# One GNN layer on one core: edge sums spilled to DRAM and scattered during the node stage

## What is computed

```
deg         = max(number of edges that end in the node, 1)
edge_weight = 1 / sqrt(deg[src] * deg[dst])
edge_msg    = relu(edge_attr @ W1e + b1e) @ W2e + b2e
messages    = (x[src] + edge_msg) * edge_weight
agg         = segment_sum(messages, dst)
h           = relu(((1 + gin_eps) * x + agg) @ W1n + b1n) @ W2n + b2n
o           = h + x
o           = o / sqrt(mean(o^2) + eps) * rms_w
out         = layernorm(x + o)
```

## Time and profile before

| | us |
|---|---|
| median of 3 runs | 1851.71 |
| lowest and highest run | 1847.68, 1855.45 |
| span of the profiled execution, first to last instruction | 1621.4 |
| between the span and the median | 230.3 |

### The profile page before, as it was taken

The page is one execution under the profiler, slowest core; times in us unless marked ns, Lnnn a source line. Parts: engine busy times, 40 slices in busy tenths (PEclk is TensorE's granted clock), DMA queues, the critical chain, the costliest instruction groups (busy, mean ns, idle before and its releaser), DMA issues. The chain is left out here.

```text
span 1621.4 us, 33827 instructions
## 1 busy us (share of the span) xinstructions
PE 1376.2 (85%) x7563; PEld 865.4 (53%) x7563; DVE 1294.2 (80%) x4160; ACT 1050.1 (65%) x3889; POOL 1309.6 (81%) x2146
## 2 busy tenths in 40 slices
PE   7995899888878888887878781499999999999993
PEld 4553455444434344443434340377777777777772
DVE  8999798767766766676666672099999999999998
ACT  7995254444444344344344342299999999999997
POOL 7777777777777777777777777369999999999997
PEclk9998899988999898899988895699999999999997
DMA  9999332222222222222222411436777777677763
GB/s 345 378 376 387 117 97 68 68 79 80 67 67 67 69 88 70 67 67 67 80 80 68 157 42 40 145 131 245 291 264 289 264 279 277 267 291 267 290 254 152
DMA packets 63860, 275.61 MB, mean 170 GB/s; under 512 B 17737, under 2 KB 20211, under 8 KB 39344
## 3 DMA queue, kind: packets, MB, share of 16 engines
q1 hardware_dynamic: 38066, 230.80, 38.1%
q0 software_dynamic: 25136, 43.60, 9.2%
q10 hardware_dynamic: 590, 0.53, 0.1%
HBM read 154.37 MB, written 128.19 MB: 174 GB/s over the span
## 5 line engine op out<-in xcount | busy, mean ns | idle before, releaser
L600 POOL DMA_INDIRECT xs<-in_x,src_x x391 | 393.5, 1006 | 119.3 <-issue 104.8
L607 POOL DMA_INDIRECT agg_scratch<-scaled,sca_i x390 | 392.8, 1007 | 118.8 <-issue 106.3
L1157 PE MATMUL bank<-digits,picks 128*128 128x512 f16 x1568 | 414.4, 412 | 0.0
L731 ACT ACTIVATE scaled<-sums,dd 128x128 f32<-128x128 f32 x390 | 124.5, 390 | 442.8 <-DMA agg_scratch<-scaled,sca_i 442.8
L641 POOL TENSOR_SCALAR xsc<-xn,rms 128x128 f32<-128x128 f32 x784 | 277.5, 371 | 61.9 <-issue 18.1
L963 DVE SCALAR_TENSOR_TENSOR sums<-sums,cont,weights 128x128 f32<-128x128 f32 x391 | 135.1, 345 | 235.8 <-issue 218.2
L943 DVE SCALAR_TENSOR_TENSOR picked<-iota_h,src_lo,bank 128x512 f16<-128x512 f16 x392 | 288.6, 737 | 9.1 <-PE bank L1157 8.2
L779 ACT ACTIVATE squares<-res 128x128 f32<-128x128 f32 x784 | 257.6, 437 | 0.0
L1157 PEld LDWEIGHTS bank<-digits,picks 128*128 128x128 f16 x1568 | 165.0, 105 | 172.5 <-issue 49.9
L655 POOL TENSOR_SCALAR on<-z,neg_mean,rstd 128x128 f32<-128x128 f32 x564 | 244.3, 443 | 0.0
L1214 PEld LDWEIGHTS bank<-w2n,hn 128*128 128x128 f32 x1568 | 205.8, 191 | 70.5 <-issue 64.6
(11 more groups left out here) (153 smaller groups left out, 2336.1 us busy)
## 6 DMA issues: line engine op xcount, KB each, us to landing
agg_scratch<-zeros SPq DMA_DIRECT2D x48, 1024.0 KB
xn<-in_x SPq DMA_DIRECT2D x48, 1024.0 KB, 8.8
out<-on SPq DMA_DIRECT2D x48, 1024.0 KB, 4.9
ag<-agg_scratch SPq DMA_DIRECT2D x47, 1024.0 KB, 6.8
highq<-src_high_scratch SPq DMA_DIRECT2D x24, 512.0 KB, 3.9
ea<-in_edge_attr SPq DMA_DIRECT2D x21, 512.0 KB, 3.7
xs<-in_x,src_x POOLq DMA_INDIRECT x391, 2.7
agg_scratch<-scaled,sca_i POOLq DMA_INDIRECT x390, 2.2
```

The lines of the kernel that those rows point to most:

```text
L600: pool.indirect_dma_start(out=xs[:, b % XS, j, :], out_offset=None, in_=x, in_offset=bass.IndirectOffsetOnAxis(ap=src_x[:, t:t + 1], axis= ...
L607: pool.indirect_dma_start(out=agg_rows, out_offset=bass.IndirectOffsetOnAxis(ap=sca_i[:, t:t + 1], axis=0), in_=scaled[:, b % SR, j, :], i ...
L1157: last = pe.matmul(ps[COUNTS[tile]][:, :], picks[:, s, c, tile * P:(tile + 1) * P], digits[:, c, :, :].rearrange("p d l -> p (d l)"), star ...
```

## The change

The edges are cut into seven groups of 56 tiles (`G`, `GT`), the group with the highest nodes first; the edge list is padded to 392 tiles. ACT no longer hands `scaled` to POOL: it stores each batch (256 KB) to a DRAM tensor `sums_scratch` with a DMA of its own queue. POOL issues all gathers in the edge stage and, beside the last 48 batches of them, 135 scatters; the others come after. A scatter reads from `reload`, two buffers of 16 tiles, which POOL fills with a plain DMA (`refill`). Behind each group comes its own join, an adding scatter of one row a partition; their sums are made on PE and scaled by ACT at the end of the edge stage.

Node blocks run from the highest nodes down. SP loads the sums of a block once as many joins have landed as the table `waits_i` says for it, which DVE computes from `dst`. For the first 98 of 196 steps (`BOTH`) POOL takes no part: DVE makes `z` straight from `xn` and `rms` in four tile operations, and `on` tiles 0 and 1; ACT makes tiles 2 and 3. From step 98 on POOL makes `xsc` and `on` as before.

The degree look-up is turned round: nodes' low parts select (two comparisons in place of four), and the sixteen matmuls of a batch have 391 columns; `picked` has 391 too. DVE's edge batches run in a loop of eight (`Fori`), PE's and ACT's too; SP's node blocks are unrolled. The run lists are made before the counting, and for all seven groups, with one round trip through DRAM (`ends_scratch`). The cut diff:

```diff
+    G, GB = 7, 14
+    GT = GB * TB
+    BATCHES = G * GB
+    T = BATCHES * TB
...
+    RB = 4 * TB
+    RELOADS = -(-T // RB)
+    EARLY = 4
...
+    LONE, ROUND = 34, SPB * XR
+    BOTH = LONE + 4 * ROUND
+    SA, SF = BOTH - 7, BOTH - 18
...
+    sums_d = nc.dram_tensor("sums_scratch", (BATCHES * P, TB * D), f32)
...
+        def act_tiles(m, w):
+            B = m // SPB
+            return (2, 3) if w < SF or isinstance(B, int) and (SPLIT <= B < BLOCKS - 2 or B == BLOCKS - 1) else (3,)
+
+        def main_tiles(m, w):
+            B = m // SPB
+            return (0, 1) if w < SF or isinstance(B, int) and B >= SPLIT else (0, 1, 2)
+
+        def late_tiles(B):
+            return (2,) if B == BLOCKS - 2 else (0, 1)
...
+            for s in range(SR):
+                sp.wait_ge(stored[s], stores(s, (G - 1) * GB))
+            sp.dma_start(tails[:, :, :], bass.AP(sums_d, ((GB - 1) * P * TB + TB - 1) * D,
+                                                 [[TB * D, P], [GB * P * TB * D, G - 1], [1, D]])).then_inc(tails_in, 16)
...
+            def load_x(i):
+                need(sp, z_ready, (i - XR + 1) * SPB)
+                sp.dma_start(xn[:, i % XR, :, :], in_group_order(x, i)).then_inc(xn_in[i % XR], 16)
+
+            def load_sums(i):
+
+                joins = sp.value_load(waits_i[0:1, i:i + 1], min_val=16, max_val=16 * G)
+                need(sp, cT_done, (i - AR + 1) * SPB)
+                sp.wait_ge(fin_added, joins)
+                sp.dma_start(ag[:, (i + 1) % AR, :, :], in_group_order(agg_d, i)).then_inc(ag_in[(i + 1) % AR], 16)
+
...
+            for i in range(XR):
+                load_x(i)
+            load_sums(0)
+            load_sums(1)
+            sp.wait_ge(msg_ready, BATCHES)
...
+            def gather(b):
+                if b == XS - TEMPS:
+                    pool.wait_ge(lists_ready, 1)
+                if b < XS - TEMPS:
+                    need(pool, counted, min(BATCHES, b * TB - COUNT_LEAD))
+                elif b < XS:
+                    need(pool, m_done, b - (XS - TEMPS) - MIX_LEAD)
+                else:
+                    pool.wait_ge(msg_ready, b - XS + 1)
...
+                for j in range(TB):
+                    t = b * TB + j
+                    pool.indirect_dma_start(out=xs[:, b % XS, j, :], out_offset=None, in_=x,
+                                            in_offset=bass.IndirectOffsetOnAxis(ap=src_x[:, t:t + 1], axis=0)
+                                            ).then_inc(xs_in[b % XF], 16)
+
+            def refill(q):
+                batches = min((q + 1) * RB, T) // TB
+                for s in range(SR):
+                    pool.wait_ge(stored[s], stores(s, batches))
+                need(pool, scattered[q % 2], 16 * scatters(q))
+                n = batches - q * RB // TB
+                pool.dma_start(reload[:, q % 2, 0:n * TB, :].rearrange("p (b j) d -> p b (j d)", j=TB),
+                               bass.AP(sums_d, q * P * RB * D, [[TB * D, P], [P * TB * D, n], [1, TB * D]])
+                               ).then_inc(reloaded[q % 2], 16)
+
+            def scatter(t):
+                q, c = t // RB, t % RB
+                if c == 0:
+                    pool.wait_ge(reloaded[q % 2], 16 * (q // 2 + 1))
+                if t % GT < GT - 1:
+                    pool.indirect_dma_start(out=agg_rows,
+                                            out_offset=bass.IndirectOffsetOnAxis(ap=sca_i[:, t:t + 1], axis=0),
+                                            in_=reload[:, q % 2, c, :], in_offset=None,
+                                            bounds_check=N - 1, oob_is_err=False).then_inc(scattered[q % 2], 16)
+                if c == RB // 2 and q + 1 < RELOADS:
+                    refill(q + 1)
+
+            def last_block(r):
+                return ((r + 1) * GT - 1) // RB
+
+            def join(r):
+
+                for k in (last_block(r), last_block(r) - 1):
+                    pool.wait_ge(scattered[k % 2], 16 * scatters(k + 2))
+                pool.wait_ge(fin_scaled, r + 1)
+                need(pool, fin_added, 16 * r)
+                pool.indirect_dma_start(out=agg_rows, out_offset=bass.IndirectOffsetOnAxis(ap=fin_i[:, r:r + 1], axis=0),
+                                        in_=joined[:, r, :], in_offset=None, bounds_check=N + P - 1,
+                                        oob_is_err=True, compute_op=ALU.add).then_inc(fin_added, 16)
...
+            BEFORE, BESIDE = 10, 135
+            for b in range(XS, BATCHES):
+                gather(b)
+                if b == XS:
+                    for k in range(ZERO_AHEAD):
+                        pool.wait_ge(agg_zeroed[k], 16 * len(range(k, ZERO_DMAS, ZERO_AHEAD)))
+                done, parts = max(b - XS - BEFORE, 0), BATCHES - XS - BEFORE
+                if b == XS + BEFORE:
+                    refill(0)
+                for t in range(done * BESIDE // parts, (done + 1) * BESIDE // parts if b >= XS + BEFORE else 0):
+                    scatter(t)
+            for t in range(BESIDE, T):
                 scatter(t)
...
+                for r in range(G - 1):
+                    if t == max(BESIDE + 12 + r, (last_block(r) + 1) * RB + 3):
+                        join(r)
+            join(G - 1)
...
+            node_step(BOTH - 1, BOTH - 1)
+            pool.wait_ge(mean_ready, SF // SPB + 1)
+            pool.wait_ge(rstd_ready, SF // SPB + 1)
+            pool.wait_ge(on_main, SF)
+            for n in range(run(pool, BOTH, 6, ROUND, node_step), STEPS + 15):
+                node_step(n, n)
...
+                m, s = b - 6, (u - 6) % SR
+                if live(m, BATCHES):
+                    act.wait_ge(scaled_ready, at(m + 1))
+                    act.dma_start(sums_d[:, :].rearrange("(b p) c -> b p c", p=P)[bass.ds(at(m), 1), :, :].rearrange(
+                        "b p c -> p (b c)"), scaled[:, s, :, :].rearrange("p j d -> p (j d)")).then_inc(stored[s], 16)
...
+                if b == BATCHES:
+                    act.wait_ge(fin_summed, EARLY)
+                    for r in range(EARLY):
+                        join_scale(r, ps[2], r)
+                if b == BATCHES + 2:
+                    act.wait_ge(fin_summed, G - 1)
+                    for r in range(EARLY, G - 1):
+                        join_scale(r, ps[3], r - EARLY)
+            act.wait_ge(fin_summed, G)
+            join_scale(G - 1, ps[7], 0)
...
+            def degree(b, u, j):
                 if j == 0:
-                    dve.wait_ge(first_counted, b + 1)
+                    dve.wait_ge(first_counted, at(b + 1))
                     need(dve, ds_ready, b - DR + 1)
                 if j == TB // 2:
-                    dve.wait_ge(second_counted, b + 1)
...
+                return dve.scalar_tensor_tensor(picked[:, j, :], iota_h[:, 0:PICK], column(src_hi, b * TB + j),
+                                                ps[COUNTS[j]][:, 0:PICK], ALU.is_equal, ALU.mult,
+                                                accum_out=deg[:, u % DR, j:j + 1])
...
+            with dve.Fori(0, 11) as i:
+
+                slot = nc.s_assert_within((i + 1) * XF - ((i + 1) * 13 >> 6) * XS, 0, XS - XF,
+                                          skip_runtime_bounds_check_because="13 * k >> 6 is k // 5 for k up to 11")
+                for u in range(10, 10 + XF):
+                    edge_step(Count(i, XF, u), u, slot + (u - 10))
+            for b in range(10 + 11 * XF, BATCHES + 4):
+                edge_step(b, b, (b - 2) % XS)
...
+            def finish(m, w, tiles, finished):
+                v, B, o, h = w % ZR, m // SPB, w // SPB % OR, w % SPB * TB
+                if h == 0:
+                    dve.wait_ge(rstd_ready, at(B + 1))
+                    dve.wait_ge(mean_ready, at(B + 1))
+                    need(dve, out_sent[o], B // OR * 16)
+                for j in tiles:
+                    last = dve.tensor_scalar(on[:, o, h + j, :], z[:, v, j, :], neg_mean[:, v // SPB, h + j:h + j + 1],
+                                             rstd[:, v // SPB, h + j:h + j + 1], ALU.add, ALU.mult)
+                last.then_inc(finished, 1)
...
                     dve.wait_ge(res_ready, at(m + 1))
-                    need(dve, z_ready, m)
-                    dve.tensor_tensor(ps[7][:, :], res[:, s, :, :].rearrange("p j d -> p (j d)"), ps[6][:, :],
+                    if both:
+                        dve.wait_ge(z_ready, at(m))
+                    q = ps[7][:, :] if both else xsc[:, s % 2, :, :].rearrange("p j d -> p (j d)")
+                    dve.tensor_tensor(q, res[:, s, :, :].rearrange("p j d -> p (j d)"), ps[6][:, :],
                                       ALU.mult).then_inc(q_ready, 1)
...
+                    need(dve, on_act, m - ZR + 1)
+                    if both:
+                        need(dve, on_main, m - ZR + 1)
+                        dve.wait_ge(xsc_ready, at(m - SA + 1))
+                        dve.tensor_tensor(z[:, v, :, :].rearrange("p j d -> p (j d)"), ps[7][:, :],
```

(58 more changed lines are left out.)

975 lines of the change are left out of this document (479 added, 496 removed).

## The result

The changed kernel takes 2060.5 us in the median of three runs (2054.6 to 2062.8), where the kernel before takes 1851.7: a ratio of 1.111, with a 95% interval of 1.106 to 1.115. It is slower by 209 us; 1648 was predicted. Its profiled execution took 2060.48 us and spans 2058.7: only 1.8 us lie around the span.

A forecast was written before the change was run, and what follows sets the result against it. POOL's gather and scatter count was taken to bound the edge stage. First `res` at 755, plus 577.7 of node stage and 85 of added DVE work, gave 1418 us of span; with 230.3 around it, 1648 (range 1600 to 1725).

The forecast's parts named there:

- The surroundings of the span: Whole run: 230.3 us between profiled span (1621.4) and median (1851.71), unexplained by any view, were carried over unchanged.
- POOL's instruction count, not its busy share, is the edge bound: Edge stage before: POOL issues without a break, 1.305 us per gather or scatter, holding messages 8.29 us apart.
- Edge pace 5.36: Edge stage after: PE sets the pace, 6.16 less 0.8 us for narrower pick matmuls, 5.36 us a batch.
- the new prelude: Before the first batch: more input DMAs and group work start batches 10 us later, bounds 3 and 20.
- Refills and POOL's count: Edge stage: 367 issues at 1.305 us and 9 refills at 2 us put POOL's last gather at about 721.
- First `res`: Turn to the node stage: join 0 at about 739, first result at 755 instead of 1044, 289 us gained.
- 98 node steps without POOL: First half of node stage: DVE takes over `z` and two `on` tiles, adding 85 us, bounds 45 and 135.
- The scatters are hidden with 20 us to spare: Beside node steps: POOL finishes 240 scatters, 15 refills, 6 joins at 1097; DVE wants `xsc` at 1117.
- (a): Rival: POOL is late at the switch to `xsc`, ending near 1190; about 1720 us, chance 0.14.
- (b): Rival: edge stage keeps 6.16 us a batch as DVE or ACT takes PE's place; 1726 us, chance 0.12.
- (c): Rival: new tiles cost 0.195 us, giving 1608; time around the span may shrink, another 29 off; chance 0.09.
- (d): Rival: slower than before, scatters beside node steps bind at 2.3 us spacing, or start waits for all joins (2006); chance 0.05.

The follow-up runs named there:

- b_same: The kernel before, unchanged, run and profiled again: 1854.7 us.
- a_480: Kernel after, 480-wide POOL write behind every scatter and gathers from batch 32, waiting for the previous write; POOL in node steps from 114: 1645.4 us, ratio 0.888 to before.
- a_every4: Kernel after, with a small POOL write and a wait for it behind each fourth gather or scatter only: 1876.0 us.
- a_drain: Kernel after, with a four-element POOL write and a wait for it behind every gather and scatter: 1749.2 us.
- a_no_late_scatters: Kernel after without its 250 scatters from tile 135 on; sums incomplete: 1751.8 us.
- a_plain_late: Kernel after, its 250 scatters from tile 135 on sent as plain POOL DMAs of the same rows to a spare tensor: 1764.7 us.
- a_long_lag1: Kernel after, with a 480-wide POOL write behind every gather and scatter, POOL waiting for the write before it: 1720.4 us, ratio 0.922 to before.
- a_240: As a_480, but writes of 240 elements and POOL taken into the node steps from step 98: 1762.8 us, ratio 0.950 to before.

## Why the prediction was wrong, point by point

**The surroundings of the span (first step): wrong.** "230.3 us lie around the span ... I carry them over unchanged." They were no overhead but stalls inside timed executions which the profiled one didn't have; b_same has 1.7 us around its span. This was the warning that I read over. Carrying them over took them as fixed; they grew with what POOL issued beside the others.

**"POOL's instruction count, not its busy share, is the edge bound": right for the profiled execution only.** In b_same POOL gets out 374 instructions in the 600 us, 1.60 us apart, and what ACT waits for is "remote". With that, relieving POOL of 255 scatters there could not give 2.93 us a batch: from b_same to the kernel after the pace didn't change at all (10.5 to 10.7 over messages 17 to 65).

**Edge pace 5.36: mechanism right, where it can be seen.** 5.40 with POOL silent, 5.39 in a_480, with PE full. That agrees with what was said of the 391 columns, though no run has 512 beside them. But the term was applied to all 98 batches. The last message came at 1084.4, not 720, of which 49 us are the late start (249.0, not 200). Against b_same's 250.0 the new prelude costs nothing, where 10 us were allowed.

**Refills and POOL's count: the issues near, the end not.** A refill's issue is 0.83 us, not 2. POOL's last gather came at 852, not 721: it waited for messages (99.9 us from 300 to 800), that is, for stalled engines. Then it stood idle for 208.8 us until join 0's row was scaled: the late scatters waited for the join though nothing in them needs it. The forecast had the two ends coincide.

**First `res`: 1100.0, not 755;** from join 0, at 1083.7, it took 16.3 us, in line with the 13.5 and the 3 for the larger load. The edge part gained 1270.2 - 1100.0 = 170 us on b_same, against 289 forecast.

**98 node steps without POOL: right in kind, and to the us by luck.** Without late scatters the stage lasts 664.1 us (1748.7 - 1084.6), 86 more than b_same's 578.1; 85 was the sum. But the first 98 steps give 76 of it: the 80 steps with two `on` tiles take 3.72 us, not 3.79. Another 11 come from the second half, 286.3 us from its first `res` to the last against 275.5 in b_same, which the forecast left as it was.

**"The scatters are hidden with 20 us to spare": this failed step decides the sign.** POOL did its 239 scatters behind join 0 in 344 us (1083.7 to 1427.9), faster than the 358 forecast and as undisturbed as its row promised. The prediction took the overlap as free: it asked only when POOL would be done, and put what the scatters cost PE, DVE and ACT at nothing. They cost 958.6 - 664.1 = 295 us, in about 14 steps. The balance against b_same closes: -170.2 + 380.5 = 210.3 us, the difference of the spans; 380.5 is 86 of work moved to DVE and 295 of stall.

Why is it so much worse than in the edge stage? There POOL has to wait for messages at every fourth gather (99.9 us from 300 to 800), which lets the others catch up; beside the node steps it hardly ever waits. This reading was not tested by itself, but a_every4 fits it, where one longer rest in four brings the node steps down to 4.5 us. The stall was already in the edge stage of both kernels, and the change moved scatters to where nothing throttles POOL.

**Rivals.** (a) names a cost of issues beside DVE, but on POOL's side; POOL was never slowed. Its "late at the switch" did appear once the stalls were cured: in a_drain DVE waits 130.5 us for `xsc`. (b), 6.16 kept, didn't occur. Of (c), the tiles are not cheaper than taken (in a_no_late_scatters 0.28 us for `z` and 0.30 for `on`, busy time over count), but the time around the span did shrink, to 1.8 us. (d) named the right sign and place, but its mechanism, spacing 2.3 us, is refuted: it was 1.29. Nor did the start wait for all joins. The trace as it was read could not show it, since in the old trace PE runs full beside the gathers from 178 to 214.

**Still open.** The mechanism. The runs fix the cause, indirect DMAs from POOL close behind each other, and the victims: PE, DVE and ACT. A rest of 0.48 us is too short in the edge stage and one of 0.68 long enough. The reloads that POOL itself waits for came in time, since it kept its 1.29 us. But no view shows the resource, and no run tells the issue of an indirect DMA from its transfers.

One candidate is the recording itself: update records go missing where POOL issues indirect DMAs, and the one trace that has nearly all of them has no stalls. The Trainium skill, NOTIFIC — the notification-queue block, section 7.1, says that the block's internal pipeline holds its producers back rather than lose a record. No run here shows that block at work, and the numbers point both ways. From 1100 to 1250 the kernel after has 366 of 1856 landings on record. a_plain_late has 3243 of 3264, nearly twice as many landings, and no stall, so their mere number isn't what stalls. a_480 lacks 1255 updates by instructions and 8674 of its 19520 landings, and has no stall either. Every run here was recorded; whether an unrecorded execution stalls was not tried.

## What to carry to other kernels

When the timed median and the profiled span differ by more than a few us, profile the kernel again before costing anything: here 230 us were the stalls that decided the case. Before moving indirect DMAs beside busy engines, ask what paces them; POOL issuing them back to back starved the others. 0.5 us of other work between two of them removed the stalls and turned a loss of 11% into a gain of 8% (a_long_lag1); with POOL's entry into the node steps moved by 16 and no writes beside the counting, the gain is 11% (a_480). And a cure that fits a theory isn't its proof: emptying the queue helped, but so did a rest with the next issue left standing in it.

## What the runs showed of the hardware

- Indirect issues 1.29 us apart (0.98 busy, 0.30 rest) slow PE, DVE and ACT from 3.8 to as much as 53 us a node step and from 5.4 to 10.7 us an edge batch. With 0.68 us of rest nothing is left of it (a_480), with 0.48 most of it in the edge stage and little in the node stage (a_240).
- In such a stretch a semaphore can rise long after the instruction that raises it: PE's matmuls ended at 1172.05, and DVE, which waited for them, started at 1190.51.
- Plain DMAs that POOL issues, 0.67 us each, do nothing of the kind (a_plain_late, steps of 3.7 us).
- 128x384 multiplications on POOL lengthen DVE's `z` tile from 335 to 534 ns; scatters leave it at 340. The 128x480 writes of a_480 leave `z` at 335 and lengthen the `on` tile from 355 to 497.
- A full wait of POOL for its own last write puts 0.77 us of idle time before the next scatter, but only 0.27 before a gather.
